# A selective scan beside attention: the summed states taken behind the scan, and the carry read from the states themselves

## The chip, the cores and the metric

One core of a Trainium2 chip runs the whole program. The metric is the device time of one execution in microseconds, the median of three runs. One further execution was recorded by the hardware profiler; the trace and the page of the profile come from it.

## The reference

Sixteen images of 64 channels by 64x64 pixels go through two layers. Layer 0 is two 3x3 convolutions with leaky ReLU and then a Mamba block over the 4096 pixels as a sequence (128 inner channels, 16 states each). Layer 1 is a channel attention and a spatial attention over the 4096 pixels, a 1x1 convolution of both and a residual. The part around the change is the selective scan:

```
def step(h, inp):
    d_t, u_t, b_t, c_t = inp
    h = jnp.exp(d_t[..., None] * A) * h + (d_t * u_t)[..., None] * b_t[:, None, :]
    y = jnp.einsum('bdn,bn->bd', h, c_t)
    return (h, y)
...
y = jnp.moveaxis(ys, 0, 1) + x * D
y = y * jax.nn.silu(z)
return y @ out_proj_w
```

Its neighbour in time is the spatial attention, softmax(q k^T) v over 4096 pixels, with exact row maxima that a search over the keys finds first.

## The kernel before

`convolutions` runs first, for all images. Then `pipeline` runs two spans of eight images. A span is a list of ticks T; every engine runs its own program over the same ticks, and semaphores order them. The order of the work in a tick is written out by hand.

A sequence is cut into 8 chunks of 512 pixels, and a chunk takes 16 ticks. The number of a tick in its chunk is r = T % 16. A tick handles 8 inner channels with their 16 states, which fill the 128 partitions. In a tick T of a scan:

- SyncE loads `lanes` (delta and delta*u, spread over the partitions) three ticks ahead (L743).
- ScalarE computes `dA` of the next tick, exp(delta*A) (L1072).
- VectorE multiplies the second half of `lanes` by B into the PSUM bank `DBU` (L1203, "the product"), and then scans dA and DBU along 512 pixels into `hst`, a ring of 24 slots of 512 floats (L1217, "the scan").
- GpSimd, one tick behind, copies the last column of the state to `carry` (L1338), from which the scan of the same channels starts 16 ticks later. Then it multiplies the state by C in place (L1345). It starts that multiplication only when VectorE's next product is through (`dbu_in`).

Beside it, in the same tick, runs the attention of an earlier image and the search of row maxima. TensorE issues, in the order of `Span.plan`: a difference matmul for the search (L863), scores in two halves (L939, L942), the matmul of the maximum (L863), the values (L953), in every second tick the sums of the softmax (L968), and then the small uses of this tick. The results of the first groups and of the small uses go into a ring of five PSUM banks: a use waits until the use five places before it has been read. ScalarE takes the difference (L1008) and the scores (L1066); VectorE takes the maximum (L1155), between its product and its scan.

Small uses have fixed ticks. In tick 2 of the next chunk TensorE sums the states of a whole chunk over the state index (L908, use "y", 16 matmuls of float32). In tick 3 VectorE adds D*u to that sum and writes `ysb` (L1195, "the summed states"). In tick 4 GpSimd gates `ysb` (L1351); in tick 7 TensorE projects it (L902). In tick 3 VectorE also ends the softplus (L1276, L1279), from which GpSimd forms `usp` (L1358). The reading of the ring's banks is counted by one semaphore for VectorE (`dve_took`), in the order of the plan: "y" stands in tick 2, ahead of the maximum of tick 3.

VectorE's order in a tick is: the summed states if r == 3 (L1192), the product (L1203), the maximum (L1208), the scan (L1217), then the extras of the tick. Before the summed states it waits for the sum of states; a wait of VectorE holds everything behind it.

The last chunk of an image hands on no carry (`carries`), and the first chunk of an image starts its scans from 0.0.

Of the kernel before, what the change touches and what calls it, by code (L numbers as in the profile page):

```python
# [19 lines left out]
ALU = mybir.AluOpType  # L20
# [78 lines left out]
def slot_of(T):  # L99

    k = T % GROUPS
    return k if k >= HALVES or T // GROUPS % 2 == 0 else k + GROUPS


class Span:
# [36 lines left out]

    def scans(self, T):
        return self.image(T // TICKS)

    def carries(self, T):

        return self.scans(T) and T >= 0 and T % TICKS < TICKS - GROUPS

    def gathers(self, T):  # L150

# [279 lines left out]
def pipeline(nc, banks, seq_d, scratch, w_in, cw, cb, w_dt_t, w_dt, dt_b, w_bc, a_log, skip,  # L431
# [4 lines left out]
    with ExitStack() as ctx:  # L436
        def sb(name, shape, dt=F32):
            return ctx.enter_context(nc.sbuf_tensor(name, shape, dt))
# [30 lines left out]
        usp = sb("usp", [P, CHUNK])  # L469
        lanes = sb("lanes", [P, SLOTS, 2, CHUNK])  # L470
        dA = sb("dA", [P, 2, CHUNK])
        hst = sb("hst", [P, HRING, CHUNK])
        carry = sb("carry", [P, GROUPS])
        ysb = sb("ysb", [P, CHUNK])

        x1c = sb("x1c", [P, 2, WIDE])
# [45 lines left out]
        with nc.Block() as block:  # L522
# [33 lines left out]
            def _(act):  # L556
# [11 lines left out]

        names = """xin_in conv tap_in tanh z_tanh gated z_gated em_in em1_in ln_in delta_in du_in st_sp
                   seq0 seq1 lanes0 lanes1 lanes2 lanes3 da_in  # L570
                   dbu_in scan carried hc_in y2_in st_x1 kd_in head_in rest_in
                   mid_in low_in st_bc ld_b ld_c abs_in st_kx st_split st_vt ring_full act_took dve_took p_full
                   pv den gathered total ld_kx0 ld_kx1 ld_kx2 ld_kx3 ld_k0 ld_k1 ld_k2 ld_k3 ld_q0 ld_q1 ld_q2 ld_q3 ld_x max_in
                   cmax cexp catt_in nm3_in nm_row acc_in den_in st_den ld_den rec_in st_rin ld_rin st_out dstep""".split()
# [2 lines left out]
        def span(j, images, tail, i):  # L577
# [45 lines left out]
            for T in range(sched.first, sched.last):  # L623
# [9 lines left out]
                    sched.note("gathered", T - 1)  # L633
                if sched.scans(T - 1):
                    sched.note("hc_in", T - 1)
                if sched.carries(T - 1):
                    sched.note("carried", T - 1)
                c, r = (T + LEAD) // GROUPS + 1, (T + LEAD) % GROUPS
                if sched.chunk(c):
                    for at, n in ((0, "xin_in"), (0, "tap_in"), (3, "conv"), (4, "tanh"), (5, "z_tanh"), (5, "gated"),  # L640
# [37 lines left out]
            with nc.Block() as block:  # L678
# [166 lines left out]
                def _(pe):  # L845
# [6 lines left out]
                    def small_use(e):  # L852
# [45 lines left out]
                        elif kind == "out":  # L898
                            if due("y2_in", c):
                                pe.wait_ge(S["y2_in"], due("y2_in", c))  # L900
                            for o in range(0, P, BLOCK):
                                mm = nc.tensor.matmul(bank[o:o + BLOCK, :], wout[:, o:o + BLOCK], ysb[:],  # L902
                                                      start=True, stop=True, tile_position=(0, o))
                        elif kind == "y":
                            wait(pe, "hc_in", GROUPS * (c + 1) - 1)
                            for gl in range(GPB):
                                for j in range(BLOCKS):
                                    mm = nc.tensor.matmul(  # L908
                                        bank[BLOCK * j:BLOCK * (j + 1), :],
                                        cst[:, C_SUM + BLOCK * gl:C_SUM + BLOCK * (gl + 1)],  # L910
                                        hst[:, slot_of(GROUPS * c + BLOCKS * gl + j), :],
                                        start=gl == 0, stop=gl == GPB - 1, tile_position=(0, BLOCK * j))
                        elif kind == "xv":
                            taken(pe, ("out", c))
                            for t in range(4):
                                for o in range(0, P, BLOCK):
                                    mm = nc.tensor.matmul(bank[o:o + BLOCK, t * P:(t + 1) * P],
                                                          x1c[:, c % 2, t * P + o:t * P + o + BLOCK], wxv[:],
                                                          start=True, stop=True, tile_position=(0, o))
                        elif kind == "en":  # L920
                            taken(pe, ("xv", c))
                            for t in range(4):
                                for o in (0, BLOCK):
                                    mm = nc.tensor.matmul(bank[o:o + BLOCK, 0:CH], xv[:, t, o:o + BLOCK],
                                                          xv[:, t, 0:CH], start=t == 0, stop=t == 3,
                                                          tile_position=(0, o))
# [208 lines left out]
                def _(dve):  # L1135
# [8 lines left out]
                    def small_use(e):  # L1144
# [35 lines left out]
                        elif kind == "en":  # L1180
# [4 lines left out]
                                ins = nc.vector.tensor_tensor(energy[:], energy[:], bank[0:CH, 0:CH], ALU.add)  # L1185
                            ins.then_inc(S["dve_took"], 1)

                    for T in range(first, last):
                        sl, r = T // GROUPS, T % GROUPS
                        ev = sched.small_uses(T)  # L1190
                        c = sl - 1
                        if sched.chunk(c) and r == 3:  # L1192
                            full_wait(dve, ("y", c))
                            full_wait(dve, ("out", c - 1))
                            nc.vector.scalar_tensor_tensor(out=ysb[:], in0=u[:, part_of(c), :], scalar=dskip, in1=bank_of(("y", c))[:],  # L1195
                                                           op0=ALU.mult, op1=ALU.add).then_inc(S["dve_took"], 1)
                        if sched.scans(T):
                            wait(dve, f"lanes{T % SLOTS}", T, 16)
                            if r == 0:
# [1 line left out]
                            if due("scan", T - 1):  # L1201
# [1 line left out]
                            nc.vector.tensor_tensor(DBU[:], lanes[:, T % SLOTS, 1, :], bbc[:, sl % 2, :],  # L1203
                                                    ALU.mult).then_inc(
                                S["dbu_in"], 1)
                        for e in ev:
                            if e[0] == "max":
                                small_use(e)  # L1208
                        if sched.scans(T):
                            g = group_of(T)  # L1210
                            if due("dbu_in", T):
                                dve.wait_ge(S["dbu_in"], due("dbu_in", T))
                            if due("da_in", T):
                                dve.wait_ge(S["da_in"], due("da_in", T))
                            wait(dve, "carried", T - GROUPS)
                            full_wait(dve, ("y", sl - 1 if T % GROUPS >= HALVES else sl - 2))
                            nc.vector.tensor_tensor_scan(  # L1217
                                hst[:, slot_of(T), :], dA[:, T % 2, :], DBU[:],
                                carry[:, g:g + 1] if sl % CHUNKS else 0.0, ALU.mult, ALU.add).then_inc(S["scan"], 1)
                        T1 = T - 1  # L1220
                        if sched.gathers(T1) and (T1 - MAIN) % KT >= 2:
                            quarter, t = sched.attends(T1), (T1 - MAIN) % KT
# [105 lines left out]
                def _(pool):  # L1328
                    for T in range(first, last):
                        sl, r = T // GROUPS, T % GROUPS  # L1330
                        if sched.scans(T - 1):
                            if r == 1:
                                wait(pool, "ld_c", sl, 16)
                            if due("scan", T - 1):
                                pool.wait_ge(S["scan"], due("scan", T - 1))
                            if sched.carries(T - 1):
                                g = group_of(T - 1)
                                nc.gpsimd.tensor_copy(carry[:, g:g + 1],  # L1338
                                                      hst[:, slot_of(T - 1), CHUNK - 1:CHUNK]).then_inc(S["carried"], 1)
                            if due("carried", T - 1):  # L1340
                                pool.wait_ge(S["carried"], due("carried", T - 1))
                            if due("dbu_in", T):
                                pool.wait_ge(S["dbu_in"], due("dbu_in", T))
                            h = hst[:, slot_of(T - 1), :]
                            nc.gpsimd.tensor_tensor(h, h, cbc[:, (T - 1) // GROUPS % 2, :],  # L1345
                                                    ALU.mult).then_inc(S["hc_in"], 1)
                        c = sl - 1
                        if sched.chunk(c) and r == 4:
# [54 lines left out]
```

## Time and profile before

| What | Value |
|---|---|
| Median of 3 runs | 7782.66 us (7779.9 to 7782.69) |
| Profiled execution: its time | 7774.7 us |
| Its span, first to last instruction | 7772.9 us |
| Busy: TensorE, VectorE, ScalarE, GpSimd | 7090.6, 6845.3, 5984.2, 3775.8 us |
| Mean granted TensorE clock | 0.972 |
| DMA engines, mean busy share in the pipeline | about 0.86 to 0.88 |

Rows of the profile read as follows. In a timeline: start in us from the start of the span, duration in us, engine, line of the code, operation, what is written <- what is read, how many instructions are merged, and in brackets how long the engine sat idle before it and what ended that. In a list of groups: line, engine, operation, forms, count | busy time in us, mean ns of one | idle time before them and its releasers. Starts of two instructions of one engine may lie closer than the duration of the first, since it still writes while the next begins; the distance from start to start is what an instruction costs the engine.

### The profile page before, as it was taken

The numbers are of one execution on the slowest core, as the hardware profiler recorded it, in microseconds if no ns is written. First come the engines' busy times: TensorE is split into PE (matmuls) and PEld (weight loads), VectorE is DVE, ScalarE is ACT, GpSimd is POOL, SyncE is SP. The second block draws the span as 40 slices with busy tenths as digits, with TensorE's granted clock in tenths as the row PEclk, the third lists the DMA queues.
The fourth block names the chain that finished last, engine by engine and source line by source line (L and its number), as shares of the span: only waits on it lengthen the run. The fifth ranks groups of instructions, "written<-read, shape, count | busy, mean of one in ns | idle before, by whom it ended". The sixth has DMA issues, their size and how long they took to land. (4 is left out here: it accounts for less than half of the span.)

```text
span 7772.9 us, 241654 instructions
## 1 busy us (share of the span) xinstructions
PE 7090.6 (91%) x92270; PEld 2794.1 (36%) x92270; DVE 6845.3 (88%) x11133; ACT 5984.2 (77%) x10710; POOL 3775.8 (49%) x4135
## 2 busy tenths in 40 slices
PE   9972389999999999999989999999999999999998
PEld 2320133333333333333333333333333333333454
DVE  2229999999999999999989999999999999999987
ACT  1115578888888888888888888888888888888875
POOL 0006655555555555555545555555555555555500
PEclk9985689999999999999999999999999999999999
DMA  9839988888898888988888888888888988889810
GB/s 152 132 78 241 241 212 213 218 206 221 202 224 206 213 213 205 223 211 213 207 206 208 214 211 208 218 212 218 208 220 204 222 206 212 215 208 222 207 42 18
DMA packets 886873, 1536.66 MB, mean 198 GB/s; under 512 B 409481, under 2 KB 459473, under 8 KB 885713
## 3 DMA queue, kind: packets, MB, share of 16 engines
q1 hardware_dynamic: 882640, 1520.79, 81.6%
q8 instruction: 728, 11.93, 0.7%
q14 instruction: 433, 3.54, 0.2%
q10 hardware_dynamic: 3072, 0.40, 0.0%
HBM read 1326.69 MB, written 176.95 MB: 193 GB/s over the span
## 5 line engine op out<-in xcount | busy, mean ns | idle before, releaser
L1345 POOL TENSOR_TENSOR hst<-hst,cbc 128x512 f32<-128x512 f32 x2048 | 2629.2, 1284 | 2202.7 <-DVE bank L1203 2174.7
L1217 DVE TENSOR_TENSOR_SCAN hst<-dA,carry,bank 128x512 f32<-128x512 f32 x1792 | 2282.4, 1274 | 5.3 <-issue 0.7
L1066 ACT ACTIVATE pr<-bank 128x512 f32<-128x512 f32 x4096 | 2222.3, 602 | 28.5 <-PE bank L942 26.8
L953 PE MATMUL bank<-pr,vt 128*32 128x512 f32 x16384 | 2154.6, 593 | 68.4 <-DVE accs L1302 67.6
L863 PE MATMUL bank<-s1kx,s1q 128*32 128x512 bf16 x16384 | 1708.6, 385 | 162.9 <-DVE mxp L1155 81.6
L1072 ACT ACTIVATE dA<-lanes,small 128x512 f32<-128x512 f32 x2048 | 1501.5, 734 | 353.5 <-DMA lanes<-spread_d 245.7
L939 PE MATMUL bank<-s1q,s1k 128*32 128x512 bf16 x16384 | 1684.8, 381 | 85.1 <-ACT gains L1008 72.0
L1008 ACT ACTIVATE gains<-bank 128x512 f32<-128x512 f32 x2048 | 1225.4, 598 | 611.2 <-DVE mxp L1155 380.2
L942 PE MATMUL bank<-t2q,t2k 128*32 128x512 bf16 x16384 | 1677.4, 380 | 0.0
L1203 DVE TENSOR_TENSOR bank<-lanes,bbc 128x512 f32<-128x512 f32 x2048 | 1537.7, 751 | 96.4 <-DMA lanes<-spread_d 11.0
L1155 DVE CUSTOM_DVE_ANT_0 gains<-bank,gains 128x512 f32<-128x512 f32 x2048 | 1399.4, 683 | 62.4 <-PE bank L863 49.9
L1338 POOL COPY carry<-hst 128x1 f32<-128x1 f32 x1792 | 726.8, 406 | 643.6 <-DVE hst L1217 642.2
L968 PE MATMUL bank<-pr,ones 128*32 128x512 f32 x7552 | 987.2, 592 | 0.0
L863 PEld LDWEIGHTS bank<-s1kx,s1q 128*32 128x32 bf16 x16384 | 508.9, 96 | 1160.1 <-issue 471.6
L939 PEld LDWEIGHTS bank<-s1q,s1k 128*32 128x32 bf16 x16384 | 513.4, 96 | 911.8 <-issue 315.5
L953 PEld LDWEIGHTS bank<-pr,vt 128*32 128x32 f32 x16384 | 554.9, 110 | 389.0 <-issue 94.6
L942 PEld LDWEIGHTS bank<-t2q,t2k 128*32 128x32 bf16 x16384 | 521.2, 97 | 294.3 <-issue 11.5
L908 PE MATMUL bank<-hst,cst 128*32 128x512 f32 x4096 | 473.8, 602 | 0.6
L968 PEld LDWEIGHTS bank<-pr,ones 128*32 128x32 f32 x7552 | 251.6, 110 | 559.9 <-issue 525.9
L400 ACT ACTIVATE biased<-bank,bias 128x512 f32<-128x512 f32 x128 | 81.1, 685 | 452.6 <-PE bank L388 440.8
L1358 POOL TENSOR_TENSOR usp<-dsp,u 128x512 f32<-128x512 f32 x128 | 213.0, 1664 | 243.8 <-DVE dsp L1279 243.8
L1217 DVE TENSOR_TENSOR_SCAN hst<-dA,bank 128x512 f32<-128x512 f32 x256 | 310.8, 1214 | 0.9 <-ACT dA L1072 0.2
(121 smaller groups left out, 5729.7 us busy)
## 6 DMA issues: line engine op xcount, KB each, us to landing
lanes<-spread_d SPq DMA_DIRECT2D x2048, 512.0 KB, 6.5
seqt<-seq_d SPq DMA_DIRECT2D x256, 128.0 KB, 5.3
spread_d<-dsp SPq DMA_DIRECT2D x128, 256.0 KB, 5.0
spread_d<-usp SPq DMA_DIRECT2D x128, 256.0 KB, 5.2
bbc<-bc_d SPq DMA_DIRECT2D x128, 256.0 KB, 5.9
cbc<-bc_d SPq DMA_DIRECT2D x128, 256.0 KB, 6.4
xpad<-in_x SPq DMA_DIRECT2D x64, 256.0 KB, 6.7
ypad<-ypad SPq DMA_DIRECT2D x128, 128.0 KB, 3.9
```

Source lines behind the costliest of these rows:

```text
L863: mm = nc.tensor.matmul(bank[o:o + BLOCK, :].rearrange("p (c n) -> p c n", n=HALF), s1q[:, q, nt * P + o:nt * P + o + BLOCK], keys[:, 2 * ...
L939: nc.tensor.matmul(bank[o:o + BLOCK, :], s1k[:, t * P + o:t * P + o + BLOCK], s1q[:, q, cols], start=True, stop=False, tile_position=(0, o))
L942: mm = nc.tensor.matmul(bank[o:o + BLOCK, :], t2k[:, t * P + o:t * P + o + BLOCK], t2q[:, q, cols], start=False, stop=True, tile_position= ...
L953: mm = nc.tensor.matmul(ACC[CH * h + o:CH * h + o + BLOCK, :], vt[:, t, o:o + BLOCK], pr[:, T % PRING, h, :], start=t == 0, stop=t == KT - ...
L968: mm = nc.tensor.matmul(DEN[o:o + 32, :], ones[:], pr[:, (2 * p + par) % PRING, h, :], start=t == 1, stop=t == KT - 1, tile_position=(0, o))
L1008: nc.scalar.activation(gains[:, k % 2, :], bank_of(e)[:], ACT.Relu).then_inc(S["act_took"], 1)
L1066: nc.scalar.activation(pr[:, T % PRING, h, :], bank_of(("S", T, h))[:], ACT.Exp).then_inc(S["p_full"], 1)
L1072: nc.scalar.activation(dA[:, (T + 1) % 2, :], lanes[:, (T + 1) % SLOTS, 0, :], ACT.Exp, scale=amat[:, g:g + 1]).then_inc(S["da_in"], 1)
L1155: nc.vector.tensor_tensor_reduce(out=gains[:, k % 2, :], in0=bank[:], in1=gains[:, k % 2, :], scale=1.0, scalar=LOWEST, op0=ALU.add, op1=A ...
L1203: nc.vector.tensor_tensor(DBU[:], lanes[:, T % SLOTS, 1, :], bbc[:, sl % 2, :], ALU.mult).then_inc(S["dbu_in"], 1)
L1217: nc.vector.tensor_tensor_scan(hst[:, slot_of(T), :], dA[:, T % 2, :], DBU[:], carry[:, g:g + 1] if sl % CHUNKS else 0.0, ALU.mult, ALU.ad ...
L1345: nc.gpsimd.tensor_tensor(h, h, cbc[:, (T - 1) // GROUPS % 2, :], ALU.mult).then_inc(S["hc_in"], 1)
```

## The change

Three edits in `pipeline`. In tick 3 VectorE runs the product, the scan, the summed states and the maximum, in that order; in the other ticks the order stays product, maximum, scan. A slot of `hst` gets 513 columns: the scan writes columns 1 to 512, GpSimd's multiplication reads columns 1 to 512 and writes columns 0 to 511, and TensorE sums columns 0 to 511. Column 512 thereby keeps the last state, and the scan of 16 ticks later takes its initial value from there; `carry`, its copy and its semaphore are gone.

```diff
-        hst = sb("hst", [P, HRING, CHUNK])
-        carry = sb("carry", [P, GROUPS])
+        hst = sb("hst", [P, HRING, 1 + CHUNK])
...
-                                        hst[:, slot_of(GROUPS * c + BLOCKS * gl + j), :],
+                                        hst[:, slot_of(GROUPS * c + BLOCKS * gl + j), 0:CHUNK],
...
+                    def summed_states(c):
+                        full_wait(dve, ("y", c))
+                        full_wait(dve, ("out", c - 1))
+                        nc.vector.scalar_tensor_tensor(out=ysb[:], in0=u[:, part_of(c), :], scalar=dskip, in1=bank_of(("y", c))[:],
+                                                       op0=ALU.mult, op1=ALU.add).then_inc(S["dve_took"], 1)
...
-                        c = sl - 1
-                        if sched.chunk(c) and r == 3:
-                            full_wait(dve, ("y", c))
-                            full_wait(dve, ("out", c - 1))
-                            nc.vector.scalar_tensor_tensor(out=ysb[:], in0=u[:, part_of(c), :], scalar=dskip, in1=bank_of(("y", c))[:],
-                                                           op0=ALU.mult, op1=ALU.add).then_inc(S["dve_took"], 1)
...
-                        for e in ev:
-                            if e[0] == "max":
-                                small_use(e)
+                        burst = r == 3 and sched.chunk(sl - 1)
+                        if not burst:
+                            for e in ev:
+                                if e[0] == "max":
+                                    small_use(e)
...
-                            wait(dve, "carried", T - GROUPS)
...
-                                hst[:, slot_of(T), :], dA[:, T % 2, :], DBU[:],
-                                carry[:, g:g + 1] if sl % CHUNKS else 0.0, ALU.mult, ALU.add).then_inc(S["scan"], 1)
+                                hst[:, slot_of(T), 1:], dA[:, T % 2, :], DBU[:],
+                                hst[:, slot_of(T - GROUPS), CHUNK:] if sl % CHUNKS else 0.0, ALU.mult, ALU.add).then_inc(S["scan"], 1)
+                        if burst:
+                            summed_states(sl - 1)
+                            for e in ev:
+                                if e[0] == "max":
+                                    small_use(e)
...
-                            if sched.carries(T - 1):
-                                g = group_of(T - 1)
-                                nc.gpsimd.tensor_copy(carry[:, g:g + 1],
-                                                      hst[:, slot_of(T - 1), CHUNK - 1:CHUNK]).then_inc(S["carried"], 1)
-                            if due("carried", T - 1):
-                                pool.wait_ge(S["carried"], due("carried", T - 1))
...
-                            nc.gpsimd.tensor_tensor(h, h, cbc[:, (T - 1) // GROUPS % 2, :],
+                            nc.gpsimd.tensor_tensor(h[:, 0:CHUNK], h[:, 1:], cbc[:, (T - 1) // GROUPS % 2, :],
                                                     ALU.mult).then_inc(S["hc_in"], 1)
```

## Rows read from the trace of the kernel before

**Rows 1.** Windows: span, busy time by engine, granted clock, DMA share, GB/s.

```profile
5000.00:6000.00 1000.00, 954.71 (x13048) 377.22 (x13044) 945.91 (x1565) 851.55 (x1534) 550.24 (x602) 1.00 0.86 212
```

**Rows 2.** VectorE's waits (us, times, longest), and line L1195 by itself (min/median/max ns).

```profile
DVE ysb L1195 <- PE bank L908: 208.5, 118, 2.7
...
L1195 DVE SCALAR_TENSOR_TENSOR ysb<-u,small,bank x128: 719/747/749, 635.4 to 7410.5; 128x512 f32<-128x512 f32 x128
```

**Rows 3.** Timeline of one tick 3, from the sum of states to tick 4.

```profile
5099.67 3.61 PE L908 MATMUL bank<-hst,cst 128*32 128x512 f32 x32
...
5100.43 1.27 DVE L1217 TENSOR_TENSOR_SCAN hst<-dA,carry,bank 128x512 f32<-128x512 f32 x1
...
5103.35 0.75 DVE L1195 SCALAR_TENSOR_TENSOR ysb<-u,small,bank 128x512 f32<-128x512 f32 x1 [1.65 <-PE bank L908]
...
5104.02 0.69 DVE L1203 TENSOR_TENSOR bank<-lanes,bbc 128x512 f32<-128x512 f32 x1
...
5104.18 0.39 PE L863 MATMUL bank<-s1kx,s1q 128*32 128x512 bf16 x4
...
5104.62 0.69 DVE L1155 CUSTOM_DVE_ANT_0 gains<-bank,gains 128x512 f32<-128x512 f32 x1
5104.85 1.29 POOL L1345 TENSOR_TENSOR hst<-hst,cbc 128x512 f32<-128x512 f32 x1 [2.90 <-DVE bank L1203]
...
5105.24 1.28 DVE L1217 TENSOR_TENSOR_SCAN hst<-dA,carry,bank 128x512 f32<-128x512 f32 x1
5105.25 0.39 PE L863 MATMUL bank<-s1kx,s1q 128*32 128x512 bf16 x4
...
5106.43 0.67 DVE L1276 TENSOR_TENSOR em<-em 128x512 f32<-128x512 f32 x1
...
5107.74 0.69 DVE L1203 TENSOR_TENSOR bank<-lanes,bbc 128x512 f32<-128x512 f32 x1
```

**Rows 4.** The same timeline, ticks 4 to 6 of that chunk.

```profile
5109.56 0.39 PE L863 MATMUL bank<-s1kx,s1q 128*32 128x512 bf16 x4
...
5109.77 1.29 POOL L1345 TENSOR_TENSOR hst<-hst,cbc 128x512 f32<-128x512 f32 x1
...
5110.33 1.28 DVE L1203 TENSOR_TENSOR bank<-lanes,bbc 128x512 f32<-128x512 f32 x1
...
5111.53 0.68 DVE L1155 CUSTOM_DVE_ANT_0 gains<-bank,gains 128x512 f32<-128x512 f32 x1
...
5114.71 0.68 DVE L1155 CUSTOM_DVE_ANT_0 gains<-bank,gains 128x512 f32<-128x512 f32 x1
```

**Rows 5.** Timeline of VectorE, ticks 4 to 6 of an image's last chunk.

```profile
3907.43 0.69 DVE L1203 TENSOR_TENSOR bank<-lanes,bbc 128x512 f32<-128x512 f32 x1
...
3908.64 1.27 DVE L1217 TENSOR_TENSOR_SCAN hst<-dA,carry,bank 128x512 f32<-128x512 f32 x1
3910.01 1.04 DVE L1203 TENSOR_TENSOR bank<-lanes,bbc 128x512 f32<-128x512 f32 x1
3910.97 0.68 DVE L1155 CUSTOM_DVE_ANT_0 gains<-bank,gains 128x512 f32<-128x512 f32 x1
...
3913.91 0.68 DVE L1155 CUSTOM_DVE_ANT_0 gains<-bank,gains 128x512 f32<-128x512 f32 x1
```

**Rows 6.** The page's costliest groups: busy us, mean ns | idle before, releaser.

```profile
L1345 POOL TENSOR_TENSOR hst<-hst,cbc 128x512 f32<-128x512 f32 x2048 | 2629.2, 1284 | 2202.7 <-DVE bank L1203 2174.7
L1217 DVE TENSOR_TENSOR_SCAN hst<-dA,carry,bank 128x512 f32<-128x512 f32 x1792 | 2282.4, 1274 | 5.3 <-issue 0.7
...
L1338 POOL COPY carry<-hst 128x1 f32<-128x1 f32 x1792 | 726.8, 406 | 643.6 <-DVE hst L1217 642.2
...
L1358 POOL TENSOR_TENSOR usp<-dsp,u 128x512 f32<-128x512 f32 x128 | 213.0, 1664 | 243.8 <-DVE dsp L1279 243.8
L1217 DVE TENSOR_TENSOR_SCAN hst<-dA,bank 128x512 f32<-128x512 f32 x256 | 310.8, 1214 | 0.9 <-ACT dA L1072 0.2
```

**Rows 7.** Groups by form: a write of the convolutions into padded rows.

```profile
L416 DVE SCALAR_TENSOR_TENSOR ypad<-biased 64x512 f32<-64x512 f32 x64 | 43.9, 686 | 197.5 <-ACT biased L400 196.5
```

More of the change, by code:

```diff
@@ L144, in scans @@
         return self.image(T // TICKS)
-    def carries(self, T):
-        return self.scans(T) and T >= 0 and T % TICKS < TICKS - GROUPS
     def gathers(self, T):
@@ L570, in pipeline @@
                    seq0 seq1 lanes0 lanes1 lanes2 lanes3 da_in
-                   dbu_in scan carried hc_in y2_in st_x1 kd_in head_in rest_in
+                   dbu_in scan hc_in y2_in st_x1 kd_in head_in rest_in
                    mid_in low_in st_bc ld_b ld_c abs_in st_kx st_split st_vt ring_full act_took dve_took p_full
@@ L635, in span @@
                     sched.note("hc_in", T - 1)
-                if sched.carries(T - 1):
-                    sched.note("carried", T - 1)
                 c, r = (T + LEAD) // GROUPS + 1, (T + LEAD) % GROUPS
@@ L1205, in _ @@
                                 S["dbu_in"], 1)
-                        for e in ev:
-                            if e[0] == "max":
-                                small_use(e)
+                        burst = r == 3 and sched.chunk(sl - 1)
[3 more added lines that the diff above has]
+                                    small_use(e)
                         if sched.scans(T):
-                            g = group_of(T)
                             if due("dbu_in", T):
@@ L1335, in _ @@
                                 pool.wait_ge(S["scan"], due("scan", T - 1))
-                            if sched.carries(T - 1):
-                                g = group_of(T - 1)
-                                nc.gpsimd.tensor_copy(carry[:, g:g + 1],
-                                                      hst[:, slot_of(T - 1), CHUNK - 1:CHUNK]).then_inc(S["carried"], 1)
-                            if due("carried", T - 1):
-                                pool.wait_ge(S["carried"], due("carried", T - 1))
                             if due("dbu_in", T):
```

## The prediction

> **What bounds the kernel now.** I read the busy time of a stretch first, then who VectorE waited for, then one chunk in order of time. In the window view [rows 1] TensorE is busy 95% and VectorE 94.6% of a stretch of 1000 us, at a granted clock of 1.00 (the 2.4 GHz level); both look full, so the shares do not say which of the two paces. The list of VectorE's waits does [rows 2]: in 7773 us it waits 208.5 us, in 118 of the 128 chunks, for TensorE's sum of states (L908) before it can take that sum (L1195), 1.77 us each time. No other wait inside the pipeline is of that size. The first and last L1195 are 635.4 and 7410.5 us, so a chunk of 16 ticks takes 53.35 us, and apart from this one stop VectorE runs nearly without a break. So VectorE sets the tick in 15 of 16 ticks, and TensorE sets the time in tick 3 of each chunk, behind its longest piece, the sum of states: 3.61 us.
>
> The timeline of one tick 3 [rows 3] shows the geometry. The scan of tick 2 starts at 5100.43 (call this s). The sum of states runs from 5099.67 to 5103.28 and VectorE takes it at 5103.35, after 1.65 us of idle. Then follow the product of lanes (5104.02), the maximum (5104.62), the scan (5105.24) and the softplus step (5106.43). Spacings from start to start: summed states 0.67, product 0.60, maximum 0.62, scan 1.19. The scores that this maximum reads are issued at 5104.18 and take 0.39, so they end at 5104.57, and the maximum starts 0.05 later: it is already as early as TensorE allows. That decides the size of the gain.
>
> **The change, part by part.**
>
> (a) The order in tick 3. After it: product, scan, summed states, maximum. The product now follows the scan of tick 2 directly and waits for that scan's signal. A row of that pairing is 3908.64 to 3910.01 [rows 5], 1.37 instead of 1.19, so 0.18 of gap. The scan now follows its own product with only a wait between; no row of before shows that pair (the maximum always covers it). Bounds: 0 from the spacing 0.60 with no gap, 0.18 from the scan-to-product pair; I take 0.18, since it too is a wait of VectorE for the instruction just in front. Then: product at s+1.37, scan at s+1.37+0.78=s+2.15, summed states at s+3.34 (the sum is ready at s+2.92: no wait), maximum at s+4.01 by VectorE alone. But its scores come at 5104.62, which is s+4.19. So it starts at s+4.19, the very time of before, with 0.18 of new idle. What stood behind it, a scan of 1.19, is done. The next step starts at s+4.19+0.62=s+4.81 in place of s+6.00: 1.19 us saved per chunk, not the 1.65 to 1.77 of the wait. Over the 118 chunks that wait: 118 x 1.19 = 140 us.
>
> Who is queued behind what: the sum's bank is freed later (s+3.34+0.75=s+4.09). TensorE needs it for the fifth use after it, the difference matmul of tick 4, at 5105.25=s+4.82 [rows 3]: 0.7 us of room. The bank of the maximum is freed when it was. The gating of ysb on GpSimd is in tick 4 and the output projection in tick 7, far behind. In the 10 chunks without the wait the two gaps cost up to 0.36 each: -4 us.
>
> On the gaps the Trainium skill disagrees: "VectorE: DVE Perf Modes", section "The DRAIN you can't avoid", says that a semaphore between two VectorE instructions costs nothing extra. The trace shows 0.18 for scan to product [rows 5]. By the page the term of -4 would be 0; the term of 140 would stay, since the scores bind there.
>
> (b) The copy of the carry is gone. It is 1792 copies of 406 ns, 726.8 us of GpSimd [rows 6]. In most ticks this is worth nothing: GpSimd's multiplication waits for VectorE's next product anyway, and the copy lies beside that product. It counts in ticks 4 to 6, where GpSimd is behind because of usp and ysb. There the multiplication of tick 3's states (5109.77 to 5111.06 [rows 4]) lies on top of VectorE's product (5110.33), which takes 1.28 instead of 0.60 to 0.70: the two exclude each other. The maximum of tick 5 starts 5111.53-5107.74=3.79 after the product of tick 4, that of tick 6 6.97 after it. A natural experiment stands in the trace: in the last chunk of an image no carry is copied. There the same distances [rows 5] are 3910.97-3907.43=3.54 and 3913.91-3907.43=6.48. So the copies cost 0.25 in tick 5 and 0.24 more in tick 6. In every second chunk the reciprocal of a quarter (L1307, L1308) lies in tick 5, GpSimd catches up meanwhile, and the product of tick 6 is not blocked: there only the first is to be had. With copies in 112 chunks, half of either kind: 56 x 0.25 + 56 x 0.49 = 41 us at most. Part of it will meet TensorE: the scores of tick 5 are there at 5109.95+0.05=s+9.57 [rows 4], and the new maximum would come at s+6.12 (the product of tick 4, 1.19 earlier than before) +3.54=s+9.66. That leaves 0.1 us of room. I take half, 20 us.
>
> (c) States one column right, product one column left. No instruction is added. VectorE writes to a start one float off in the convolutions already (L416, 512 elements), at the usual price: 686 ns [rows 7], where the product of 512 elements takes 0.69 us [rows 3]. For GpSimd no row shows such an operand. Lower bound 0 (1284 ns stays [rows 6]); upper bound see the third rival. I take 0, because all its operands stay runs of 512 floats. The scan's initial value stays one float per partition from SBUF; its wait for the carry was never the last.
>
> Sum: 140 - 4 + 20 = 156 us. The profiled execution took 7774.7 us (span 7772.9), so 7619; the median of the three runs is 8.0 us above it, so 7627 us.
>
> **The rivals.**
>
> 1. *TensorE paces part of it.* For: it is idle only 45.29 of 1000 us [rows 1], 2.4 us per chunk, and after the change 1.19 to 1.5 of it is gone. Its sum of states and the scores behind it must come that much earlier in every chunk. If some of the idle time hangs on chains of its own (the scores of tick 5 have 0.1 us of room), the rest returns as waits of the maximum for scores. Against: much of its idle time is waiting for VectorE, which now comes sooner, and 2.4 is more than 1.5. If half of term (a) returns and (b) is lost: 70 - 4 = 66 us, 7774.7 - 66 + 8 = 7717 us.
>
> 2. *Hidden anyway.* The wait moves whole to the next maximum. This needs the scores of tick 3 more than a scan later than they are; the row says 0.18. 7783 us, within 0.2%.
>
> 3. *Slower: GpSimd's shifted multiplication.* It reads at a start that is one float off and writes into the run that it reads. In the shortest ticks it starts 0.83 behind a product's start (5104.02 to 5104.85 [rows 3]) and the next product comes at 0.60+0.62+1.37=2.59, so there is room for 1.76 us; now it takes 1284 ns. The nearest dearer row of GpSimd is usp with 1664 ns [rows 6], which contains blocking. From about 1.76 on, every product of VectorE is blocked: at twice the time, 2.57, it is 0.81 x 14 ticks x 128 = 1450 us, some 9080 us. Already at 1.72 three crowded ticks pay 0.44 each, 3 x 0.44 x 128 = 169 us, which eats the gain: 7796 us, and that is the point from which it decides. Against: nothing in the rows links a start address to a time, on any engine.
>
> 4. *It does not do what it says*: the scan stalls on its initial value, taken from the row of states. That value is 16 ticks old, and for half the slots lies in the row being overwritten. A cost of 0.06 us per scan (the difference of the forms with and without carry, 1274 and 1214 ns [rows 6]) would be 1792 x 0.06 = 108 us, 7735 us. Against: it is the same kind of operand as before.
>
> **How the numbers follow.** Forecast 0.62, at 7627: from 7580 (all of (b), and TensorE drawn along, so that VectorE's own path counts, 1.77-0.36=1.41 per chunk: 166+41-4=203 off) to 7665. Rival 1: 0.20, 7665 to 7765. Rival 4: 0.04, faster still. Rival 2: 0.06. Rival 3: 0.06, and 0.02 for other losses. The range of 8 in 10 leaves out the far side of rivals 1 to 3: 7580 to 7725. A measurement of this kernel tells about 0.2% (16 us) from no change. Faster by more: 0.62+0.20+0.04=0.86; same 0.06; slower 0.06+0.02=0.08.
>
> **What would show each step.** In the changed kernel's list of waits L1195's 208.5 us is nearly gone, and the maximum's wait for the scores grows by about 118 x 0.18 = 21 us; if it grows by over 80, rival 1 is right. In a timeline of tick 3 product to scan is 0.72 to 0.78 and scan to summed states 1.19. In ticks 5 and 6 the blocked products take 1.04, not 1.28. GpSimd's multiplication still has a mean of 1284 ns and its copies are gone; a higher mean is rival 3. The scan's mean stays at 1274; more is rival 4. A chunk takes about 52.1 us. The prediction is wrong above all if TensorE's scores, in any of ticks 4 to 9, come later than VectorE's new pace allows.

## The result, and the profile after

The changed kernel takes 7607.4 us (median), the kernel before 7781.5: a ratio of 0.9775, interval 0.9759 to 0.9791, or 163 to 188 us less. One of its four executions took 11407.9 us, at a mean granted clock of 0.606, and is in the median (7606.0 without it) but not in the ratio. Measured again, the ratio came to 0.9778 (0.9765 to 0.9792). The profiled execution took 7608.85 us with a span of 7606.4.

The numbers of lines have moved: the product is L1196 now, the maximum L1148, the scan L1210, the summed states L1184, GpSimd's multiplication L1337, the sum of states L901, the search scores L856. First VectorE's waits of the changed kernel (us, times, longest), beside [rows 2]:

```profile
DVE gains L1148 <- PE bank L856: 102.1, 233, 2.8
...
DVE ysb L1184 <- PE bank L901: 5.0, 17, 0.6
DVE ysb L1184 <- PE bank L856: 3.6, 1, 3.6
```

The wait for the sum, 208.5 us in 118 pieces, is 5.0 us in 17. The maximum's wait for scores is twice what it was; its row of before was

```profile
DVE gains L1155 <- PE bank L863: 49.9, 105, 2.8
```

Then the window view, beside [rows 1]: VectorE is busy 96.5% instead of 94.6%, TensorE 96.7% instead of 95.5%, both at a granted clock of 1.00; the DMA engines rose from 0.86 to 0.89.

```profile
5000.00:6000.00 1000.00, 967.13 (x13364) 406.18 (x13360) 964.69 (x1607) 872.54 (x1576) 423.83 (x343) 1.00 0.89 217
```

The costliest groups by line, beside [rows 6]. The copy is gone. The scan costs what it did (1276 against 1274 ns), the product's mean fell from 751 to 730 ns, and GpSimd's multiplication, with the same number of elements, from 1284 to 1187 ns:

```profile
L1337 POOL TENSOR_TENSOR hst<-hst,cbc 128x512 f32<-128x512 f32 x2048 | 2430.2, 1187 | 3418.1 <-DVE bank L1196 3417.4
L1210 DVE TENSOR_TENSOR_SCAN hst<-dA,hst,bank 128x512 f32<-128x512 f32 x1792 | 2286.3, 1276 | 8.4 <-DVE bank L1196 0.6
...
L1196 DVE TENSOR_TENSOR bank<-lanes,bbc 128x512 f32<-128x512 f32 x2048 | 1495.5, 730 | 115.7 <-DMA lanes<-spread_d 17.6
```

Last, a timeline of tick 3, beside [rows 3]:

```profile
5046.60 3.65 PE L901 MATMUL bank<-hst,cst 128*32 128x512 f32 x32
...
5047.16 1.28 DVE L1210 TENSOR_TENSOR_SCAN hst<-dA,hst,bank 128x512 f32<-128x512 f32 x1
5048.54 0.70 DVE L1196 TENSOR_TENSOR bank<-lanes,bbc 128x512 f32<-128x512 f32 x1
5049.28 1.28 DVE L1210 TENSOR_TENSOR_SCAN hst<-dA,hst,bank 128x512 f32<-128x512 f32 x1
...
5050.47 0.72 DVE L1184 SCALAR_TENSOR_TENSOR ysb<-u,small,bank 128x512 f32<-128x512 f32 x1
...
5051.11 0.43 PE L856 MATMUL bank<-s1kx,s1q 128*32 128x512 bf16 x4
...
5051.58 0.69 DVE L1148 CUSTOM_DVE_ANT_0 gains<-bank,gains 128x512 f32<-128x512 f32 x1 [0.39 <-PE bank L856]
...
5052.20 0.69 DVE L1274 TENSOR_TENSOR em<-em 128x512 f32<-128x512 f32 x1
```

The sum of states ends at 5050.25, and VectorE comes for it at 5050.47: no wait. The scores end at 5051.54, and the maximum, with nothing left to do ahead of it, waits 0.39 us for them. Scan to product is 1.38, product to scan 0.74.

### The profile page after: what moved, and what is told of

It reads as the page before. It is cut to its first block and busy times, and to the rows that moved or that the text cites. A ratio compares the mean times of both kernels' runs of the same rounds, so it can differ in the third digit from the quotient of the medians.

```text
span 7606.4 us, 237965 instructions
## 1 busy us (share of the span) xinstructions
PE 7027.0 (92%) x92270; PEld 2922.8 (38%) x92270; DVE 6809.0 (90%) x11133; ACT 5966.1 (78%) x10710; POOL 2859.6 (38%) x2343
## 5 line engine op out<-in xcount | busy, mean ns | idle before, releaser
L1337 POOL TENSOR_TENSOR hst<-hst,cbc 128x512 f32<-128x512 f32 x2048 | 2430.2, 1187 | 3418.1 <-DVE bank L1196 3417.4
L1210 DVE TENSOR_TENSOR_SCAN hst<-dA,hst,bank 128x512 f32<-128x512 f32 x1792 | 2286.3, 1276 | 8.4 <-DVE bank L1196 0.6
L856 PE MATMUL bank<-s1kx,s1q 128*32 128x512 bf16 x16384 | 1732.1, 384 | 63.3 <-DVE mxp L1148 19.8
L935 PE MATMUL bank<-t2q,t2k 128*32 128x512 bf16 x16384 | 1694.5, 379 | 0.0
L1196 DVE TENSOR_TENSOR bank<-lanes,bbc 128x512 f32<-128x512 f32 x2048 | 1495.5, 730 | 115.7 <-DMA lanes<-spread_d 17.6
L1148 DVE CUSTOM_DVE_ANT_0 gains<-bank,gains 128x512 f32<-128x512 f32 x2048 | 1403.0, 685 | 116.4 <-PE bank L856 102.1
L856 PEld LDWEIGHTS bank<-s1kx,s1q 128*32 128x32 bf16 x16384 | 529.5, 96 | 937.3 <-issue 471.4
L932 PEld LDWEIGHTS bank<-s1q,s1k 128*32 128x32 bf16 x16384 | 536.7, 96 | 875.6 <-issue 328.6
L946 PEld LDWEIGHTS bank<-pr,vt 128*32 128x32 f32 x16384 | 576.4, 110 | 392.5 <-issue 92.8
L935 PEld LDWEIGHTS bank<-t2q,t2k 128*32 128x32 bf16 x16384 | 540.2, 97 | 295.7 <-issue 10.8
L901 PE MATMUL bank<-hst,cst 128*32 128x512 f32 x4096 | 473.7, 601 | 0.6
L1350 POOL TENSOR_TENSOR usp<-dsp,u 128x512 f32<-128x512 f32 x128 | 212.8, 1662 | 420.6 <-DVE dsp L1277 420.6
L1210 DVE TENSOR_TENSOR_SCAN hst<-dA,bank 128x512 f32<-128x512 f32 x256 | 311.3, 1216 | 1.3 <-ACT dA L1065 0.2
L1245 DVE SCALAR_TENSOR_TENSOR cacc<-xin,small,cacc 128x512 f32<-128x512 f32 x384 | 278.4, 725 | 9.7 <-ACT cacc L1088 9.5
```

Of the source, the lines that this page charges most:

```text
L856: mm = nc.tensor.matmul(bank[o:o + BLOCK, :].rearrange("p (c n) -> p c n", n=HALF), s1q[:, q, nt * P + o:nt * P + o + BLOCK], keys[:, 2 * ...
L932: nc.tensor.matmul(bank[o:o + BLOCK, :], s1k[:, t * P + o:t * P + o + BLOCK], s1q[:, q, cols], start=True, stop=False, tile_position=(0, o))
L935: mm = nc.tensor.matmul(bank[o:o + BLOCK, :], t2k[:, t * P + o:t * P + o + BLOCK], t2q[:, q, cols], start=False, stop=True, tile_position= ...
L946: mm = nc.tensor.matmul(ACC[CH * h + o:CH * h + o + BLOCK, :], vt[:, t, o:o + BLOCK], pr[:, T % PRING, h, :], start=t == 0, stop=t == KT - ...
L1148: nc.vector.tensor_tensor_reduce(out=gains[:, k % 2, :], in0=bank[:], in1=gains[:, k % 2, :], scale=1.0, scalar=LOWEST, op0=ALU.add, op1=A ...
L1210: nc.vector.tensor_tensor_scan(hst[:, slot_of(T), 1:], dA[:, T % 2, :], DBU[:], hst[:, slot_of(T - GROUPS), CHUNK:] if sl % CHUNKS else 0. ...
```

## The experiments

**The order alone.** The kernel before, with only this of the change:

```diff
-                        if sched.chunk(c) and r == 3:
-                            full_wait(dve, ("y", c))
...
+                        burst = r == 3 and sched.chunk(sl - 1)
+                        if not burst:
+                            for e in ev:
+                                if e[0] == "max":
+                                    small_use(e)
...
+                        if burst:
+                            summed_states(sl - 1)
+                            for e in ev:
+                                if e[0] == "max":
+                                    small_use(e)
```

> Only the order of tick 3 is changed (product, scan, summed states, maximum); the carry and its copy stay. Theory (the maximum of tick 3 is bound by its scores, a scan of 1.19 us comes ahead of it): 118 x 1.19 - 4 = 136 us off, 7645 us, ratio 0.9825; the wait of the summed states for the sum falls from 208.5 to under 15 us. Rival (TensorE paces part of it): 60 to 100 us off, with the maximum's wait for scores over 130 us in total. Rival (the copy's removal made most of the 174 us): under 60 us off.

Measured: 7658.5 us, ratio 0.9848 (0.9835 to 0.9862), so 120 us less. Of VectorE's waits in it:

```profile
DVE gains L1155 <- PE bank L863: 94.2, 208, 2.8
...
DVE ysb L1191 <- PE bank L908: 4.9, 16, 0.6
```

The mechanism is right, the size 16 us too large. The rows add up to the gain: the wait for the sum went from 214.9 to 8.5 us (-206), the maximum's wait from 49.9 to 94.2 (+44), and the two gaps cost (1.38-1.19)+(0.74-0.60)=0.33 us in each of 128 chunks (+42). That makes -120.

Where the 16 us went shows in the distance from the scan of tick 2 to the product of tick 4, taken in each of the 128 chunks. In 104 of them it is 1.17 us shorter on average (122 us together), the scan that was foretold. In 14 it is only 0.52 shorter (7 us): that is the second chunk of an image, in which VectorE had waited 0.81 us for the sum and not 1.92 as in the 104. In the ten chunks without the wait it is 0.11 longer. Together 128 us. Of the rise of the maximum's wait 35.5 us lie in tick 3; the other 9 lie in other ticks and are lost. One second chunk, before:

```profile
4020.55 1.28 DVE L1217 TENSOR_TENSOR_SCAN hst<-dA,carry,bank 128x512 f32<-128x512 f32 x1
...
4022.63 0.75 DVE L1195 SCALAR_TENSOR_TENSOR ysb<-u,small,bank 128x512 f32<-128x512 f32 x1 [0.81 <-PE bank L908]
...
4027.02 0.69 DVE L1203 TENSOR_TENSOR bank<-lanes,bbc 128x512 f32<-128x512 f32 x1
```

and with the new order:

```profile
3964.37 1.28 DVE L1219 TENSOR_TENSOR_SCAN hst<-dA,carry,bank 128x512 f32<-128x512 f32 x1
...
3970.26 0.69 DVE L1203 TENSOR_TENSOR bank<-lanes,bbc 128x512 f32<-128x512 f32 x1
```

That is 6.47 us before and 5.89 after, 0.58 earned.

**The columns alone.** The changed kernel with the order of before; the diff is the part on `hst` and `carry` of the one above.

> Only the columns and the carry are changed; the order of tick 3 stays as before. Theory (the copies cost only where GpSimd's multiplication blocks VectorE's product): 174 - 136 = 38 us off, 7743 us, ratio 0.995, with the blocked products of ticks 5 and 6 at 1.04 us or less in place of 1.28, and 208.5 us of waiting for the sum unchanged. Rival (copies hidden anyway): no change, 7781. Rival (the two parts help each other): under 20 us off here although 174 together.

Measured: 7722.9 us, 0.9935 (0.9922 to 0.9949), 55 us less, and the wait for the sum stands at 209.0 us. The two parts give 120 + 55 = 175, and together they gave 174: they neither help nor hinder each other. The product's busy time fell by 42 us (1537.7 to 1496.0), which is the 41 us that the prediction had as its upper end for the copies. The other 13 us stand in a second instruction that GpSimd blocks. In every second chunk a short addition in front of the reciprocal (L1307, here L1298) lies in tick 5, where the product of tick 6 would otherwise be blocked:

```profile
L1307 DVE TENSOR_TENSOR rq<-dq 128x8 f32<-128x8 f32 x64 | 56.1, 877 | 4.8 <-DMA dq<-den_d 4.8
```

and in the kernel with the columns alone

```profile
L1298 DVE TENSOR_TENSOR rq<-dq 128x8 f32<-128x8 f32 x64 | 41.2, 644 | 4.8 <-DMA dq<-den_d 4.8
```

It takes 14.9 us less over the kernel. From scan to scan, tick 5 and tick 6 each became some 28 us shorter in sum, 0.25 us in nearly all of the 112 chunks with copies.

**The summed states behind the product only.** Before, with the order product, summed states, maximum, scan.

```diff
-                        if sched.chunk(c) and r == 3:
-                            full_wait(dve, ("y", c))
...
                                 S["dbu_in"], 1)
+                        if r == 3 and sched.chunk(sl - 1):
+                            summed_states(sl - 1)
                         for e in ev:
                             if e[0] == "max":
                                 small_use(e)
```

> Before, with the summed states behind the product instead of behind the scan: product, summed states, maximum, scan. Theory (the scores of tick 3 bind the maximum, only what is moved ahead of the maximum is earned, and the product stood ahead of it already): no gain, 7775 to 7785 us, ratio 0.999 to 1.001; the wait for the sum falls by about 0.6 to 0.78 us per chunk (to some 130 us) and the maximum's wait grows by as much. Rival (whatever covers the wait is earned): 118 x 0.6 = 70 us off, 7711 us, ratio 0.991.

Measured over eleven runs: 7779.6 us, ratio 1.0003 (0.9994 to 1.0011). Nothing is earned, although almost half of the wait is gone:

```profile
DVE ysb L1191 <- PE bank L908: 115.0, 103, 1.9
DVE gains L1155 <- PE bank L863: 114.7, 225, 2.8
```

The wait for the sum fell by 93.5 us and the maximum's wait rose by 64.8. The gap between the scan of tick 2 and the product, 0.19 us in each of 128 chunks, takes 24 of the remaining 29. This is the sharpest test of the step on which the prediction rests: the next thing that VectorE needs from TensorE is 1.29 us behind the sum, so covering the first wait with work that stood ahead of the second one anyway is worth nothing. Only the scan, which came from behind the maximum, is earned.

**One column right, in place, with the copy.** Before, with slots of 513 floats; source and target of GpSimd's multiplication are both columns 1 to 512.

```diff
-        hst = sb("hst", [P, HRING, CHUNK])
+        hst = sb("hst", [P, HRING, 1 + CHUNK])
...
-                            h = hst[:, slot_of(T - 1), :]
+                            h = hst[:, slot_of(T - 1), 1:]
```

> Before, with slots of 513 floats, states in columns 1 to 512 and GpSimd's multiplication in place there (source and target the same columns), carry copied as before. It asks why the multiplication takes 1090 ns in two of four ticks of the changed kernel. Theory A (the place of the run in memory modulo 16 bytes decides): a pattern of four ticks here too, with some at about 1090 ns. Theory B (a target one float below the source decides): 1284 ns in all ticks. Theory C (the copy in front slows it): 1284 ns in all ticks here, but 1090 in the kernel with columns only also in ticks of both kinds.

Measured: 7781.9 us (one run, before 7778.1: no difference that a single run could show), and the multiplication has a mean of 1187 ns here too. From GpSimd's timeline (the multiplications of the states of ticks 2, 3, 4 and 5 of a chunk):

```profile
4028.18 1.09 POOL L1345 TENSOR_TENSOR hst<-hst,cbc 128x512 f32<-128x512 f32 x1 [2.06 <-DVE bank L1203]
...
4033.11 1.28 POOL L1345 TENSOR_TENSOR hst<-hst,cbc 128x512 f32<-128x512 f32 x1
...
4036.30 1.28 POOL L1345 TENSOR_TENSOR hst<-hst,cbc 128x512 f32<-128x512 f32 x1
...
4038.28 1.09 POOL L1345 TENSOR_TENSOR hst<-hst,cbc 128x512 f32<-128x512 f32 x1
```

Theory A holds: the place decides. A slot is 2052 bytes, so its start moves by 4 bytes modulo 16 from slot to slot, and the time follows with a period of four: slots 0 to 3 of the ring are slow, fast, fast, slow (the rows above begin with a slot of the kind of 2). It is the same in place and with the target one float lower, so by these two kernels it is the source's place that counts. The faster half earns nothing here: the two multiplications that block VectorE's product are those of states 3 and 4, which are the slow ones. The run also separates the copies from the faster multiplication: with the copies the product's busy time stayed at 1536.1 us, and with the same multiplication times but no copies (the columns alone) it was 1496.0.

**Two columns right.** The changed kernel, with every slot at the same, fast place (the columns of the scan and of the sum of states move along):

```diff
-        hst = sb("hst", [P, HRING, 1 + CHUNK])
+        hst = sb("hst", [P, HRING, 4 + CHUNK])
...
-                            nc.gpsimd.tensor_tensor(h[:, 0:CHUNK], h[:, 1:], cbc[:, (T - 1) // GROUPS % 2, :],
+                            nc.gpsimd.tensor_tensor(h[:, 1:1 + CHUNK], h[:, 2:2 + CHUNK], cbc[:, (T - 1) // GROUPS % 2, :],
...
```

> The changed kernel with slots of 516 floats and every column of the states one further right (GpSimd reads columns 2 to 513, writes 1 to 512), so that every slot stands to 16 bytes as slots 1, 5, 9 ... of the changed kernel do, where the multiplication took 1090 ns. Theory (place modulo 16 bytes sets the time, and the two crowded multiplications hold VectorE's product): all multiplications near 1090 ns, the products of ticks 5 and 6 blocked for 0.19 and some 0.3 us less, 20 to 40 us off the changed kernel: some 7575 us. Rival (faster multiplication is hidden, as in the kernel with the states one column right in place, which took 7781.9): 7600 to 7612 us.

Measured: 7586.4 us, 0.9754 (0.9741 to 0.9768); all 2048 multiplications took 1082 to 1122 ns, and the product's mean fell to 714. That is 21 us less than the changed kernel, the low end of what was expected. Both were measured again, side by side.

> The changed kernel once more, on the same chip as the next two, so that small distances can be told: 0.9775 to 0.9785 of before.

> The kernel with the columns two right once more: if GpSimd's faster multiplication is worth what the drop of the product's busy time says (1495.5 to 1462.9 = 33 us, part of it eaten by the maximum's wait), it is 15 to 30 us faster than the changed kernel in the same call; if it is hidden, under 8 us.

Measured: 7605.4 us for the changed kernel, 7585.7 for the columns two right, 20 us apart. So the faster multiplication is worth something once the two that block VectorE are fast too. The product's busy time fell by 33 us; part of it went into the maximum's wait (102.1 to 112.0).

**The maximum behind both softplus steps.** The changed kernel, with the maximum of tick 3 moved once more.

```diff
                         if burst:
                             summed_states(sl - 1)
-                            for e in ev:
-                                if e[0] == "max":
-                                    small_use(e)
...
+                        if burst:
+                            for e in ev:
+                                if e[0] == "max":
+                                    small_use(e)
                         done = sched.ended(T)
```

> The changed kernel with the maximum of tick 3 also behind the two softplus steps of that tick. It covers the idle time that is left ahead of this maximum (0.24 and 0.39 us in two chunks). Theory: 118 x 0.3 = 35 us off the changed kernel, some 7572 us, since the bank of this maximum is needed only 1.3 us later than it is then free. Rival (freeing the maximum's bank and the gains buffer 1.3 us later holds TensorE and ScalarE in ticks 4 and 5): no gain or a loss of up to 60 us.

Measured: 7625.2 us, 0.9804 (0.9791 to 0.9818): 18 to 20 us slower than the changed kernel, and not for the reason that the rival gave. The maximum's wait did fall, from 102.1 to 56.3 us, and TensorE's waits hardly moved. What rose is VectorE's own product:

```profile
5009.35 0.69 DVE L1274 SCALAR_TENSOR_TENSOR dsp<-dtx,em 128x512 f32<-128x512 f32 x1
5009.96 0.68 DVE L1148 CUSTOM_DVE_ANT_0 gains<-bank,gains 128x512 f32<-128x512 f32 x1
5010.12 1.28 POOL L1351 TENSOR_TENSOR usp<-dsp,u 128x512 f32<-128x512 f32 x1 [2.33 <-DVE dsp L1274]
...
5010.57 1.39 DVE L1196 TENSOR_TENSOR bank<-lanes,bbc 128x512 f32<-128x512 f32 x1
```

delta (L1274) releases GpSimd's usp. With the maximum behind it, usp starts before the product of tick 4 and holds it until 5011.40; in the changed kernel the product came right behind delta, and usp was the one that had to wait (1662 ns on average, 1306 here). In tick 5 the product is held longer as well (1.33 us on average, 1.08 in the changed kernel). The product's busy time rose from 1495.5 to 1595.4 us, which is more than the 46 us saved. The Trainium skill ("SBUF — State Buffer", section "SBUF: two separate sides") calls this an exclusive lock that goes to whichever starts first, for the whole instruction. The trace agrees: beside a usp that had started first the product took 1.39 us instead of 0.69.

**The maximum between the two softplus steps**, on top of the columns two right: summed states, em, maximum, delta, so that delta stays right ahead of the product.

```diff
...
                                 link(nc.vector.tensor_tensor(em1[:], em1[:], em[:], ALU.subtract))
+                                if burst:
+                                    for e in ev:
+                                        if e[0] == "max":
+                                            small_use(e)
...
```

> The kernel with every column two right, and the maximum of tick 3 between the two softplus steps (L1272 and L1279 of that kernel's order: summed states, em, maximum, delta). The first step (0.70 us) covers the 0.39 and 0.46 us that this maximum waits for its scores, and delta, which releases GpSimd's usp, still stands right ahead of the product of tick 4, so no new blocking. Theory: 118 x 0.35 = 41 us off the kernel with the columns two right (7586), some 7545 us; the maximum's wait falls to under 60 us and the product's mean stays near 714 ns. Rival (as when the maximum stood last: each later maximum costs elsewhere what it saves): 7580 us or more.

Measured: 7568.4 us, 0.9733 (0.9720 to 0.9747), 17 us faster than the columns two right alone, the fastest version here. The place worked: in the timeline the maximum of tick 3 waits no more, and the product's mean was 708 ns, no higher than the 714 beside it. But 41 us were expected, and the reason shows in one row:

```profile
DVE gains L1148 <- PE bank L856: 129.4, 324, 2.8
```

It was 112.0 us in 278 pieces in the kernel beside it. What tick 3 gave, later ticks took back in part. In tick 3 the maximum's wait fell from 40.0 to 0.5 us, in tick 5 it rose from 3.0 to 46.7 (104 times), in tick 8 from 12.0 to 28.0. A maximum of tick 5:

```profile
5023.79 0.69 DVE L1148 CUSTOM_DVE_ANT_0 gains<-bank,gains 128x512 f32<-128x512 f32 x1 [0.47 <-PE bank L856]
```

So VectorE now comes too early for the scores of tick 5, those for which the prediction had counted 0.1 us of room: here TensorE begins to pace, its first rival.

**The short sum, in both kernels.** To see how much TensorE paces, only the first 4 of 16 matmuls of the sum of states are issued, 2.6 us less per chunk (the result lacks three quarters of the states).

```diff
-                            for gl in range(GPB):
+                            for gl in range(1):
```

> The changed kernel with only the first quarter of the matmuls of the sum of states (4 of 16; the result of the scan layer is therefore wrong): TensorE has 2.6 us less to do per chunk. It asks how much TensorE still paces. Theory (VectorE paces; only its waits for scores are left, 102.1 us, of which some 60 came behind the sum): 40 to 70 us off the changed kernel, 7540 to 7570 us. Rival (TensorE paces part of every chunk): over 100 us off.

> The kernel before with the same three quarters of the matmuls left out. The wait for the sum should be gone (0.9 us instead of 3.6 behind the same start), so all of it is earned: 208.5 us off, some 7572 us, that is 30 to 55 us (the copies, less the 0.33 us of gaps per chunk that the new order brings) from the changed kernel with the short sum. Rival (the wait is caused by something ahead of the sum, not its length): under 120 us off.

Measured: 7589.0 us (0.9753, 0.9740 to 0.9766) for the changed kernel and 7606.0 (0.9781, 0.9768 to 0.9795) for the one before. So with 2.6 us less work on TensorE in each of 128 chunks, 333 us, the changed kernel gains 16 to 18 us, not the 40 to 70 that were expected. Its busy time fell by 259 us only (7027.0 to 6767.9). The kernel before gains 171 us instead of 208.5, and the two lie 17 us apart instead of 30 to 55. The short sum opens other waits. In the kernel before, one tick 3 with the short sum:

```profile
5094.52 1.03 PE L908 MATMUL bank<-hst,cst 128*32 128x512 f32 x8
...
5098.57 1.28 ACT L1117 ACT_TABLE_LOAD   x1
...
5099.98 0.58 ACT L1008 ACTIVATE gains<-bank 128x512 f32<-128x512 f32 x1
...
5100.61 0.40 PE L939 MATMUL bank<-s1q,s1k 128*32 128x512 bf16 x4 [2.69 <-ACT gains L1008]
...
5101.86 1.93 PE L953 MATMUL bank<-pr,vt 128*32 128x512 f32 x8
...
5106.97 0.69 DVE L1155 CUSTOM_DVE_ANT_0 gains<-bank,gains 128x512 f32<-128x512 f32 x1 [1.29 <-PE bank L863]
```

ScalarE is busy with the logarithm (L1116) and its two table loads, and TensorE's next scores wait until ScalarE has read a bank of the ring (L1008). In the kernel before, the same table loads and logarithm (5100.70 to 5103.92) lie beside the long sum of states (5099.67 to 5103.28). Over the whole kernel these scores' wait for L1008 is 248.4 us with the short sum and 72.0 without. In the changed kernel TensorE waits in the same place for the summed states instead (178.3 us, 118 times), whose bank is freed later. So the short sum is no clean removal of one load. It shows that the sum's length is not worth 333 us to the changed kernel; how far TensorE's own pace lies below is left open.

## Why the prediction was right, step by step

The forecast was 7627 us (7580 to 7725), the measured time 7607.4.

*The order, (a).* The place and the mechanism held: the gain is the scan that is taken out from behind the maximum, and the run with the summed states behind the product shows it from the other side, at 1.0003. The term was 140 - 4 us and is 120. The geometry was read from one chunk, in which the maximum started 4.19 us behind the scan of tick 2. In other chunks its scores come later, 4.42 us behind that scan in the chunk of the timeline above, and the maximum waits 0.39 us there. That costs nothing, since before the change the maximum started equally late in that chunk:

```profile
5047.03 1.27 DVE L1217 TENSOR_TENSOR_SCAN hst<-dA,carry,bank 128x512 f32<-128x512 f32 x1
...
5051.45 0.69 DVE L1155 CUSTOM_DVE_ANT_0 gains<-bank,gains 128x512 f32<-128x512 f32 x1
```

So the scan's 1.19 us hold in both, 1.17 on average, and the gaps are hidden behind the scores, as the working said. What was mis-sized is the count. Of the 118 chunks 14 had waited only 0.81 us, and there VectorE's own path sets the time: about the wait less the two gaps is earned. And some 9 us return as waits for scores in other ticks, for which the sum had nothing. For the maximum's wait +21 us were foretold; +44 came with the order alone and +52 in the changed kernel. The cost of the gaps was taken as 0.36 per chunk and is 0.33: 0.19 from scan to product, 0.14 from product to scan.

*The bank of the sum.* At the search matmuls TensorE's wait for the summed states is 0.6 us in the changed kernel, in two pieces: the 0.7 us of room was there.

*The copies, (b).* The upper end, 41 us, was read from the last chunks of an image, where nothing is copied, and it is the 42 us by which the product's busy time fell. Halving it for fear of TensorE's scores in tick 5 was wrong: by the run of this part alone the gain is 55 us, and beside the new order still 51 (7658.5 to 7607.4). The upper end itself was too low. It gave every second chunk nothing for tick 6, since the product is not blocked there; but the addition in front of the reciprocal was blocked in its place, and lost 14.9 us of its time in the columns alone. The blocked products take 1.03 to 1.05 us in most chunks of the changed kernel, as foretold.

*The columns, (c).* The cost of 0 for VectorE held (1276 ns a scan). The extra time of GpSimd's multiplication was bounded from below at 0, and it went below: 97 ns faster on average. No row of before spoke for that; it changed no time here, since the two multiplications that count are in slow places.

So 16 us too much in one term and 35 too little in the other made a sum that is 19 us short. The range held through the mechanism, the closeness of the middle partly through luck: the two errors have opposite signs.

*The rivals.* TensorE's pace: the maximum's wait grew by 52 us, more than the 21 foretold and less than the 80 that were to show this rival; it takes some 9 us of term (a) and is plain two steps further on, with the maximum between the softplus steps. Hidden anyway: the time excludes it, and the kernel with the product alone ahead shows what it looks like. GpSimd slowed by the shift: the opposite. The scan's initial value from its own row: no cost.

## What to carry to other kernels

When a wait is to be covered, look for the second thing that the waiting engine needs from the same source, and how far behind the first it comes. Only work that moves in front of that second point is earned; here it was the scan, 1.19 us of a wait of 1.77, and nothing when the product was used for it. Where the wait itself is shorter than that, less is earned. Before moving an instruction, ask also what its neighbour releases: a producer that stood right ahead of the instruction it will collide with should stay there. When a blocking instruction becomes shorter, look for every instruction that it had blocked, not only for the costliest. And read the geometry in each kind of chunk, not in one.

## What the runs showed of the hardware

GpSimd's elementwise multiplication of 128x512 float32 takes about 1090 or 1285 ns by the place of its source modulo 16 bytes. Counted from the start of `hst`, sources at 8 and 12 are fast and sources at 0 and 4 slow. In slots of 2052 bytes the two kinds alternate in pairs; in slots of 2064 bytes, with the source at 8, it is 1082 to 1122 ns for all 2048 instructions; in the slots of 2048 bytes of before, with the source at 0, it is 1258 to 1302. Where `hst` itself starts was not read, and a run with the other source, `cbc`, moved was not made: whether the address or the distance of the two sources counts is open. The Trainium skill ("GPSIMD Engine Reference", section 3.1) gives about 2.6 cycles per element at 1.2 GHz; worked out, an estimate of 1109 ns. The fast place agrees; the slow one is 16% above.

TensorE's granted clock fell after a pause of 2.69 us. In the kernel before with the short sum, TensorE had idled that long behind ScalarE; then the values matmul took 1.93 us instead of 1.03. In the windows of this kernel (columns as in [rows 1]) the clock is 1.00, the level of 2.4 GHz, up to 5100, and 0.69 on average in the next 5.5 us, so part of them at 1.2 GHz:

```profile
5094.00:5100.00 6.00, 3.92 (x52) 1.22 (x44) 6.00 (x11) 4.65 (x8) 2.55 (x2) 1.00 1.02 232
5100.00:5105.50 5.50, 4.89 (x48) 1.42 (x52) 4.75 (x7) 4.22 (x9) 4.13 (x3) 0.69 0.81 194
```

So less work for TensorE made its later work dearer, and the mean clock of that kernel is 0.963, against 0.972 in the kernel before.
